# Layer 2's products for three of eight contraction tiles as fp32r products of halves, with low halves made by accumulating transfers

## What is computed

```python
x = x + x @ W0.T + 0.5 * (x @ A0[label]) @ B0.T           # layer 0, one W0 for all batches
x = x + quantise(x, thresholds, deltas, zero_points)      # layer 1, eight levels of a mask and a candidate
x = x + x @ W2[adapter].T                                 # layer 2, a 1024x1024 matrix chosen per batch
x = x + (x @ B3[adapter].T) @ A3[adapter].T               # layer 3, rank 16
```

## Time and profile before

| | us |
|---|---|
| median of 3 | 464.55 (464.13 to 465.97) |
| profiled execution | 464.56 |
| its span | 462.7 |
| TensorE busy | 454.7 (98%) |
| VectorE busy | 415.4 (90%) |
| ScalarE busy | 326.7 (71%) |
| DMA, hardware queue | 62.4 MB, 37.5% of 16 engines |

### The profile page before, as it was taken

How to read it: one execution, slowest core, us unless ns; L and a number is a source line. 1 busy time by engine, 2 the same in 40 slices (tenths; PEclk the granted TensorE clock), 3 DMA queues, 4 the chain that set the end, 5 groups by cost and what they waited for, 6 DMA issues and landing times.

```text
span 462.7 us, 7306 instructions
## 1 busy us (share of the span) xinstructions
PE 454.7 (98%) x3006; PEld 410.9 (89%) x3006; DVE 415.4 (90%) x395; ACT 326.7 (71%) x274; POOL 8.1 (2%) x18
## 2 busy tenths in 40 slices
PE   7999999999999999999999999999999999999995
PEld 7899999889998899889998899989998899988884
DVE  4889999999699996999699996999869999999983
ACT  5699979958398747967398754996349848665730
POOL 1000000000000000000000000100000000000000
PEclk9999999999999999999999999999999999999999
DMA  7983430557128534367227543183322522245242
GB/s 279 343 334 104 91 103 1 91 188 279 69 92 221 196 142 159 69 204 279 76 91 188 197 174 126 48 261 132 120 92 91 181 92 96 75 173 180 94 159 91
DMA packets 17941, 69.15 MB, mean 149 GB/s; under 512 B 2421, under 2 KB 3445, under 8 KB 13045
## 3 DMA queue, kind: packets, MB, share of 16 engines
q1 hardware_dynamic: 17044, 62.41, 37.5%
q0 software_dynamic: 864, 6.29, 7.3%
HBM read 54.01 MB, written 8.39 MB: 135 GB/s over the span
## 4 chain that ended last, share of the span: by engine, by line
PE 90%; DMA 3%; issue 2%; DVE 2%; SPq 2%; ACT 1%; DVEq 0%; ACTq 0%
PE l_ps L838 39%; PE l_ps L773 37%; PE l_ps L853 6%; PE bx_ps L872 2%; PE l_ps L783 2%; DMA w_sb<-w 2%; PE bx_ps L799 2%; DMA adapter_ids<-adapters 1%; PE l_ps L902 1%; PE bx_ps L806 1%; PE bx_ps L879 1%; DVE quant L628 1%; ACT cand L439 0%; ACT magnitude L429 0%; SPq L287 0%
## 5 line engine op out<-in xcount | busy, mean ns | idle before, releaser
L838 PE MATMUL l_ps<-x,w_sb 128*128 128x256 f32 x896 | 196.9, 380 | 0.4 <-DVE x L595 0.4
L838 PEld LDWEIGHTS l_ps<-x,w_sb 128*128 128x128 f32 x896 | 169.2, 190 | 25.3 <-issue 2.8
L634 DVE COPY_PREDICATED quant<-mask,cand 128x2048 f32<-128x2048 int8 (+2 forms) x77 | 145.6, 1891 | 0.4
L439 ACT ACTIVATE cand<-x,inv_delta 128x2048 f32<-128x2048 f32 (+2 forms) x88 | 134.5, 1528 | 8.8 <-DVE quant L628 7.0
L449 ACT ACTIVATE mask<-magnitude,thr_bias 128x2048 fp8e5<-128x2048 f32 (+2 forms) x77 | 117.7, 1529 | 13.4 <-DVE quant L634 12.7
L608 DVE TENSOR_SCALAR cand<-cand,delta 128x2048 f32<-128x2048 f32 (+2 forms) x88 | 87.9, 999 | 10.1 <-ACT cand L439 9.8
L616 DVE TENSOR_SCALAR cand<-cand,lower,upper 128x2048 f32<-128x2048 f32 (+2 forms) x88 | 93.4, 1062 | 0.4
L773 PE MATMUL l_ps<-x_hi,w_hi 128*128 128x256 f32 x512 | 87.1, 292 | 0.9 <-DVE x_lo L565 0.9
L773 PE MATMUL l_ps<-x_hi,w_lo 128*128 128x256 f32 x512 | 82.8, 283 | 0.0
L773 PE MATMUL l_ps<-x_lo,w_hi 128*128 128x256 f32 x512 | 82.5, 283 | 0.0
L773 PEld LDWEIGHTS l_ps<-x_hi,w_hi 128*128 128x128 f32 x512 | 71.4, 191 | 6.6 <-issue 4.2
(11 more groups left out here) (66 smaller groups left out, 231.0 us busy)
## 6 DMA issues: line engine op xcount, KB each, us to landing
w_sb<-w SPq DMA_DIRECT2D x31, 1024.0 KB, 4.9
out<-x SPq DMA_DIRECT2D x32, 256.0 KB, 2.2
x_raw<-x SPq DMA_DIRECT2D x15, 512.0 KB, 6.4
x_lo<-x_raw POOLq DMA_DIRECT2D x6, 1024.0 KB, 8.2
a_raw<-a SPq DMA_DIRECT2D x8, 512.0 KB, 3.6
w_sb<-w SPq DMA_DIRECT2D x7, 512.0 KB, 7.4
b_sb<-b SPq DMA_DIRECT2D x8, 256.0 KB, 2.7
a_raw<-a SPq DMA_DIRECT2D x8, 128.0 KB, 6.3
```

The costliest lines, as they stand in the source:

```text
L439: act.activation(cand[:, c % CANDS, 0:n], x2_unit(u), ACT.Identity, bias=ROUND, scale=inv_delta[:, k:k + 1]).then_inc(rounded, 1)
L634: dve.copy_predicated(y, mask[:, m % MASKS, 0:n].bitcast(I8), t).then_inc(merged, 1)
L838: last = nc.tensor.matmul(l2_bank(b, q)[:, i * S:(i + 1) * S], w2_tile(b, o)[:, k * P:(k + 1) * P], x2[:, b % SLOTS, k * S:(k + 1) * S], s ...
```

## The change

For batches 0 to 6, contraction tiles 0 to 2 of layer 2 (EDGE = 3) are computed with nine fp32r products of halves in place of three float32 products; tiles 3 to 7 stay float32. In the order of TensorE's program two fp32r products stand behind each of the first four float32 products, and the ninth behind the fifth. Batch 7 stays wholly float32.

- The high and the negated half of each output tile's three weight tiles (128 x 384) are written by ScalarE (`split_w2`, two operations for each of eight output tiles, spread over `between`); GpSimd's queue adds the raw weights with an accumulating DMA (`add_w2`, 192 KB, 56 of them). There are four buffers of halves, so `split_w2` of output tile o waits until TensorE has finished tile o-4.
- The halves of x2 (128 x 768) are made by ScalarE (`split_x2` in `between(u, 1)` of the next unit, so behind `candidate` 2) and VectorE (`split_x2` at the end of the unit, behind the four `finish`). TensorE's `layer2` waits for the latter.
- W2 is loaded by output tile, in one part for tiles 3 to 7 (128 x 640) into a ring of five and one for tiles 0 to 2 into a ring of three.
- To make room, other tensors share buffers: the staging of W0 uses the candidate buffers, A3's raw data the upper half of x3 (so that `load_a3` waits for two stores to land), `low_parts` and `bx_parts` become one, and the last batch's loads go to free halves of cand, quant and magnitude.

```diff
+EDGE = 3
+SPLIT = B - 1
+RING = 5
+RAW = 3
+HALVES = 4
@@ gpsimd
+            def add_w2(b, o):
+                pool.wait_ge(w2_neg_done, T * b + o + 1)
+                pool.dma_start(lo_tile(b, o), edge_tile(b, o), accum_op=ALU.add).then_inc(w2_added[o], 16)
+            add_x(2)
+            for o in range(HALVES):
+                add_w2(0, o)
+            for s in range(1, B):
+                if s + 2 < B:
+                    add_x(s + 2)
+                for o in range(HALVES, T):
+                    add_w2(s - 1, o)
+                if s < SPLIT:
+                    for o in range(HALVES):
+                        add_w2(s, o)
@@ scalar
+            def split_w2(b, o):
+                n = T * b + o
+                act.wait_ge(w2_edge_loaded[o], (b + 1) * 16)
+                if n >= HALVES:
+                    act.wait_ge(l2_done, n - HALVES + 1)
+                act.activation(hi_tile(b, o), edge_tile(b, o), ACT.Copy).then_inc(w2_hi_done, 1)
+                act.wait_ge(w2_hi_done, n + 1)
+                act.activation(lo_tile(b, o), hi_tile(b, o).bitcast(F32), ACT.Copy, scale=-1.0).then_inc(w2_neg_done, 1)
+            def split_x2(b):
+                act.wait_ge(x2_done, x2_count(b))
+                if b > 0:
+                    act.wait_ge(l2_done, T * b)
+                act.activation(x2_hi[:, :], x2[:, b % SLOTS, 0:EX], ACT.Copy).then_inc(x2_hi_done, 1)
@@ scalar, between(u, j), units of batches 1 to 6 (s)
-                    if j == 1 and s + 2 < B:
-                        split_batch(s + 2)
+                    if j == 1:
+                        split_x2(s - 1)
+                        if s + 2 < B:
+                            split_batch(s + 2)
+                    if j == 2:
+                        split_w2(s - 1, 4)
+                        split_w2(s - 1, 5)
                     if j == 3:
+                        split_w2(s - 1, 6)
                         split_a3(s - 1)
+                    if j == 5 and s < SPLIT:
+                        split_w2(s, 0)
+                        split_w2(s, 1)
                     if j == 6:
                         drain_l0(s + 1, 0)
+                        if s < SPLIT:
+                            split_w2(s, 2)
+                            split_w2(s, 3)
@@ scalar, quantise
                 for j in range(1, G):
                     test(u, j)
+                    if j == 4 and 0 < UNITS[u][0] < B - 1:
+                        split_w2(UNITS[u][0] - 1, 7)
@@ vector
+            def split_x2(b):
+                dve.wait_ge(x2_hi_done, b + 1)
+                dve.tensor_tensor(x2_lo[:, :], x2[:, b % SLOTS, 0:EX], x2_hi[:, :].bitcast(F32),
+                                  ALU.subtract).then_inc(x2_split_done, 1)
@@ vector, end of quantise(u)
                     for q in range(4):
                         finish(UNITS[u][0] - 1, q)
+                if UNITS[u][0] < SPLIT and u > 0:
+                    split_x2(UNITS[u][0])
@@ tensor, layer2(b, q)
+                if q == 0:
+                    pe.wait_ge(x2_split_done, b + 1)
                 for i in range(2):
                     o = 2 * q + i
+                    dst = l2_bank(b, q)[:, i * S:(i + 1) * S]
+                    pe.wait_ge(w2_loaded[o], (b + 1) * 16)
+                    pe.wait_ge(w2_added[o], 16 * (b + 1))
+                    for k in range(EDGE, T):
+                        last = nc.tensor.matmul(dst, w2_block(b, o, k), x2[:, b % SLOTS, k * S:(k + 1) * S],
+                                                start=(i == 0 and k == EDGE), stop=False)
+                        if k == T - 1:
+                            last.then_inc(w2_used, 1)
+                        for n in range(2 * (k - EDGE), min(2 * (k - EDGE) + 2, 3 * EDGE)):
+                            term, e = divmod(n, EDGE)
+                            w = lo_tile(b, o) if term == 2 else hi_tile(b, o)
+                            v = x2_lo if term == 1 else x2_hi
+                            last = nc.tensor.matmul(dst, w[:, e * P:(e + 1) * P], v[:, e * S:(e + 1) * S],
+                                                    start=False, stop=(i == 1 and n == 3 * EDGE - 1))
+                    last.then_inc(l2_done, 1)
@@ sync, load_a3 for 0 < b < B - 1
+                    sp.wait_ge(out_stored[2], 16 * b)
+                    sp.wait_ge(out_stored[3], 16 * b)
```

More of the change, by code:

```diff
@@ new lines, in _ @@
+            for s in range(1, B):
+                for o in range(RING, T):
+                    load_w2(s - 1, o, adapter)
+                load_edge(s - 1, T - 1, adapter)
+                adapter = adapter_of(s)
+                if s < B - 1:
+                    for o in range(RING):
+                        load_w2(s, o, adapter)
+                        if o == 1 and s + 3 < B:
+                            load_batch(s + 3)
+                        if o < RAW:
+                            load_edge(s, o, adapter)
+                    for o in range(RAW, T - 1):
+                        load_edge(s, o, adapter)
+                else:
+                    for o in range(RING):
+                        load_edge(s, o, adapter)
+                    load_w2(s, 0, adapter)
+                    for o in range(RING, T):
+                        load_w2(s, o, adapter)
+                        load_edge(s, o, adapter)
+                    load_a3(s, adapter)
+                    for o in range(1, RING):
+                        load_w2(s, o, adapter)
+                load_b3(s, adapter)
+                for q in range(4):
@@ L315, in _ @@
                     store(s - 1, q)
+                if s < B - 1:
+                    load_a3(s, adapter)
+            for q in LAST_ORDER:
+                store(B - 1, q)
             for q in range(4):
@@ L496, in between @@
                         drain_l0(s, 1)
+                    if j >= 4:
+                        split_w2(s - 1, j)
                 elif u == LAST + 2:
@@ L805, in sum_low @@
                 pe.wait_ge(low_parts_done, b + 1)
-                nc.tensor.matmul(bx_ps[:, S:2 * S], low_sum[:, :], low_parts[:, :], start=True, stop=True)\
+                nc.tensor.matmul(bx_ps[:, S:2 * S], low_sum[:, :], parts[:, :], start=True, stop=True)\
                   .then_inc(low_sum_done, 1)
@@ L857, in last_layer2 @@
                     if part == len(PARTS) - 2:
-                        last.then_inc(l2_done, 1)
+                        last.then_inc(l2_done, 2)
             def low_rank3(b, q):
@@ L871, in low_rank3 @@
                     rows = slice(k % n * w, (k % n + 1) * w)
-                    last = nc.tensor.matmul(bx_ps[rows, 0:S], b3_sb[:, k, 0:w], x3[:, k * S:(k + 1) * S],
+                    last = nc.tensor.matmul(bx_ps[rows, 0:S], b3_tile(b, k, w), x3[:, k * S:(k + 1) * S],
                                             start=(k < n), stop=(k >= T - n))
@@ L878, in sum_bx @@
                 pe.wait_ge(bx_parts_done, b + 1)
-                nc.tensor.matmul(bx_ps[:, S:2 * S], bx_sum[:, :], bx_parts[:, :], start=True, stop=True)\
+                nc.tensor.matmul(bx_ps[:, S:2 * S], bx_sum[:, :], parts[:, :], start=True, stop=True)\
                   .then_inc(bx_sum_done, 1)
```

207 lines of the change are left out of this document (123 added, 84 removed).

## The result

| | before | after |
|---|---|---|
| median, us | 464.54 | 510.2 (507.99 to 512.43) |
| ratio, 95% interval | | 1.098 (1.092 to 1.104) |
| profiled execution, its span, us | 464.56, 462.7 | 512.43, 510.6 |

The account below looks back on a forecast made before the run. TensorE was taken as the bound, VectorE about 4 us behind. Products and seam, with other waits, gave a span of 481; 5.5 for transfers, 4 for the clock and 1.9 outside the span made 492 us, range 474 to 506.

Parts of the forecast that it names:

- What bounds the kernel: Kernel before: TensorE is the bound, busy 98% of 462.7 us, with VectorE only about 4 us behind.
- part 1: Layer 2's products on TensorE: an output tile goes from 3.48 to 3.25 us, 12.6 us less for seven batches.
- Part 2, the seam: TensorE ahead of layer 2: permission comes 13.3 us after sum_bx starts, against 10.3 now, so 3.0 us wait each round.
- Part 3, the accumulating transfers: TensorE at tile 4: transfer takes about 4 us, has 3.3; 0.8 us late each round, 5.5 over the rounds.
- Rival C: Accumulating transfers beside W2's loads make tiles 4 and 7 late by over 2 us a round: from 505; chance 0.14.
- Part 4, the clock: TensorE's clock falls after the gaps ahead of layer 2: 4 us lost in all, bounds 0 to 16.
- What is free: Shared buffers, SyncE's added issues and TensorE's added waits except tile 4 cost nothing; ScalarE is tight but not the limit.
- other waits: Ahead of layer 2: 5.4 us in the first round; drain_l0 at batches 4 and 5 adds 2.7 and 6.6 us.
- the forecast's seam alone: Whole kernel with products, seam and the other waits, without transfers and clock: a span of 481 us.
- The sum: Whole kernel: 481 + 5.5 + 4 = 490.5 us of span, plus 1.9 us outside it: 492.
- Rival B: At the seam, ScalarE reaches split_x2 in time (under 10.3 us from sum_bx), TensorE stays the bound: 452; chance 0.09.
- Rival D: Seam costs less than it looks because both engines shift; the two sides cancel: 463 to 478; chance 0.07.

Follow-up runs that it names:

- E7: Changed kernel with ScalarE's split_x2 moved behind candidate 0 of the next unit and no accumulating transfers (low halves inexact): 466.06 us, 1.005.
- E9: E7 with the nine fp32r products of each output tile grouped behind its five float32 ones: 468.55 us in one run.
- E12: Kernel before, layer 2 wholly float32, plus only split_x2 on ScalarE and VectorE and TensorE's wait for it, halves unused: 502.2 us, 1.081.
- E2: Changed kernel without the 56 accumulating transfers; low halves stay negated high halves, so layer 2 is inexact: 499.99 us, 1.077.
- E5: Changed kernel with the next batch's x load issued behind all of W2's pieces instead of behind the second: 501.67 us, 1.082.
- E3: Changed kernel with filler products keeping TensorE busy in the gaps ahead of layer 2, results unchanged: 519.47 us, 1.112.
- E4: Changed kernel with both no accumulating transfers (low halves inexact) and filler products in the gaps ahead of layer 2: 494.35 us, 1.064.
- E11: E10 without the accumulating transfers (low halves inexact): 471.63 us, 1.014.
- E10: Changed kernel, all computed, with split_x2 behind candidate 0, x loaded late, and ScalarE's split_w2, split_batch and drain_low order tuned: 477.01 us, 1.025.

## Why the prediction held or fell, step by step

*What bounds the kernel, and part 1: right.* The output tile was put at 3.25 us and takes 3.22. E7's layer 2 to `sum_bx` fell from 42.43 to 40.52 us, 1.9 where 1.8 was forecast. The 120 ns for an fp32r product, taken from its neighbour, measured 118, whichever order it stands in. The Trainium skill's rule in "TensorE: Matmul & The Clock Gate", section "Back-to-back issue gap", quoted in the prediction as 109 ns, shows in neither E7 nor E9. The section gives that rule for an isolated gap. For a real stream of weight loads and products it has 81 ns at 128 columns and 131 at 512. The measured 118 lies between the two, but a straight line between them, an estimate of ours from these two figures, would have given 98, so neither part of the section has the number, and the pitch taken from this kernel's own rows was the one that held.

*Part 2, the seam: right.* 13.3 us from `sum_bx` to layer 2 was forecast and 13.39 came; for batches 4 and 5 it is 16.09 and 19.94, 2.7 and 6.55 over the plain one, where 2.7 and 6.6 were forecast. The first start is 86.03 for 86.2. VectorE's idle time of 5.70 us ahead of `split_x2`, released by ScalarE, is the sign that was named for it. E12 shows the seam by itself, and E7 against E2 shows it taken away but for 2.04 us. They give 38 and 34 us with the clock's part, against 481 - 462.7 + 12.6 = 30.9 and 4 for the clock in the prediction.

*Part 3, the accumulating transfers: wrong in the sentence "Tiles 5 to 7 are on time once tile 4 is."* The work for tile 4 was near: TensorE wanted it 14.1 us after layer 2's start (14.0 forecast), and GpSimd issued it 9.2 us after (10.7 forecast, when the 1.9 us of the split are taken off both). It waited in only one of six rounds, although in rounds 1 to 5 its transfer took 4.3 to 5.7 us, not 3.7: ScalarE was 1.5 us earlier than forecast. Tile 7 was never worked out. It is issued 20.1 us after the start and wanted at 172.19 - 2.42 - 143.98 = 25.8, so it has 5.7 us, more than the 3.7 that a transfer was put at. It took 7.6 to 9.1 us to land. The term was sized at 3.7 us from the means of other transfers, and what SyncE had in flight beside it was not asked. E5 shows that this is the cause: with the x load elsewhere the same transfers take 3.1 to 4.2 us, and tile 7's waits in the rounds are gone with 8.5 us. The waits for transfers come to 13.7 us where 5.5 were put, and leaving the transfers out gives back 10.2. Rival C had the mechanism (tile 4 and then 7, beside W2's loads) but named W2's loads and not x's. Its chance of 0.14 was too low. That its 505 to 513 hold the result is partly luck: C gets there by transfers alone, while without any transfer the kernel still takes 500 (E2). The last batch adds 4.3 us of waits (1.06, 0.45 and 2.79), where ScalarE splits one tile a step (`j >= 4`). This was not worked out either.

The Trainium skill, "DMA: Bandwidth & Descriptors", section on the SWDGE path, would have 2.45 us for such a transfer. The measured median is 4.3 us, the shortest 3.0, and beside the x load it is 7.6 to 9.1. The measurement decides. No run here has a plain copy of this size in that queue, so how much of the difference is due to accumulating stays open.

*Part 4, the clock: right in kind, too small.* The granted clock did fall to the 1.2 GHz level, at six of TensorE's waits of 2.4 us and more, and stayed at the 2.4 GHz level at three others (2.96, 3.31 and 2.79 us). But a fall lasts 3.4 to 10.2 us, not the 4 for which none of the prediction's rows had a figure, and 14.3 us of TensorE's time are lost on the timeline where 4 were put. What comes back when it is held is less. With the transfers in place it is nothing (E3), since TensorE then waits longer for tile 7. Without them it is 5.6 us (E2 to E4): rounds 2 to 4 go from 42.0 to 42.3 us to 41.1 between layer 2 and `sum_bx`, and round 1 loses 2.5 to the wait in the next point. The bounds of 0 to 16 held it.

*What is free, and other waits: one missed.* The prediction followed `drain_l0` at the ends of batches 4 and 5 but not in round 1. There ScalarE's `drain_l0` waits for VectorE's last `drain_l2`, VectorE's unit starts late behind ScalarE's added splits and waits again for candidates within it, and so layer 0's bank is emptied late. TensorE waits 1.34 us at it in E2, 3.53 in E4, 4.48 in E7 and 5.70 in E11, and 1.43 in E12, where only the seam was added. In the changed kernel the transfers and the clock delay TensorE by more than this, so it is not seen. The same holds for `sum_bx` in the last batch (2.0 to 2.1 us). This is why the forecast's seam alone (481 of span) was never reached: E4, which is nearest to it, has 493.7. (The prediction also gives ScalarE 3.4 us of idle time before `test` 2. In the kernel before, a steady round has none there; nothing in the sum rests on it.)

*The sum.* The measured time is 18 us over the forecast's 492. The steps that failed are three terms: the transfers, the clock, and `drain_l0` in round 1 with `sum_bx` at the end, which were put at nothing. Read on the timeline, transfers and clock take 20 us more than allowed and fill the gap by themselves. Taken away one after the other, they give another split: the transfers 10.2 us where 5.5 were allowed (E2), then the clock 5.6 where 4 were (E4), and 494.35 - 483 = 11 us stay, for ScalarE's copies and the clock at them (6.3 + 4.5). That last part is hidden in the changed kernel and is the largest miss of the three by this order. Rival B, TensorE as the bound at 452, needs more than its stated condition: E7 meets it in rounds 2 to 4 and still stands at 466, because TensorE, once its own path is shorter, runs into ScalarE's copies. Rival D is out; both sides came close to their full price.

What stays open: how much of the missed waits in E7 and E11 is ScalarE's own work and how much comes by way of VectorE; by how much each of the two 512 KB loads lengthens an accumulating transfer, and whether their issue order or their bytes do it. E5 moves both at once. Nor was `add_x` moved away from tile 6 in E10's order, nor the change tried with more than four buffers of halves.

## What to carry to other kernels

An operation put into an in-order queue is paid at the place where the bounding engine waits for it, not by its own length: 1.8 us of splitting a round cost 34 to 38 us in all, since 9.4 us of ScalarE's other work stood ahead of it in every round. Before a product is made cheaper, ask how far the other engines are behind: here 1.9 us was gained in each of three rounds and nothing arrived, since VectorE was only some 4 us behind TensorE, and in the first round, the fifth and at the end TensorE met copies that ScalarE makes behind its splits and behind VectorE. For every transfer with a deadline, write down issue time, deadline and what else is issued within a few us of it, on either queue, for the last of a series as well as for the first.

## What the runs showed of the hardware

- An accumulating transfer of 192 KB from the software queue took 4.3 us at the median of 56 and 3.0 at the least. Where two loads of 512 KB were issued within 0.9 us of it, it took 7.6 to 9.1 us (changed kernel); the same four without those loads took 3.1 to 4.2 (E5). Issued 3.5 to 4.3 us behind a 1 MB accumulating transfer of its own queue, it took 8.1 to 9.6 us (E10).
- TensorE's granted clock stood at 0.50 for 3.4 to 10.2 us at six of its waits of 2.4 to 9.5 us in the changed kernel (up to 13.7 us in E5), and at 1.00 behind others of up to 3.31 us. Holding it up by filler work gave nothing back where another wait followed (519 for 510 us) and 5.6 us where none for a transfer did.
- Products of fp32r with a weight load each come every 118 ns for 256 columns in a group (E9), and an output tile takes 3.23 us grouped and 3.22 mixed with float32 instructions.
